# Batch 0's first maxima moved ahead of batch 1's set-up, six transfers moved to ScalarE, and the first experts' indirect transfers without bounds

## The reference, cut to what matters

```python
x = x + tanh(g_xattn[0]) * attention0(layernorm(x), ctx)   # 16 heads of 16, causal, softmax
x = x + tanh(g_ffn[0])   * experts0(layernorm(x))          # top 8 of 32 experts, 256 slots each
x = x + tanh(g_xattn[1]) * attention1(layernorm(x), ctx)   # 16 heads of 16, masked, softmax
x = x + tanh(g_ffn[1])   * experts1(layernorm(x))          # top 2 of 8 experts, 1024 slots each
```

## Time and profile before

| what | value |
|---|---|
| median of 3 executions | 1957.07 us |
| the profiled execution's own time | 1959.72 us |
| its span | 1958.0 us |
| PE busy | 1784.8 us (91%) |
| DVE, ACT, POOL busy | 1006.0, 887.7, 788.7 us |
| granted TensorE clock, mean | 0.97 |
| first attention | span from 0 to about 580 us |
| first experts | about 580 to 828 us |
| second attention, second experts | from 828 us to the end |

### The profile page before, as it was taken

One profiled execution on the slowest core, in us unless ns is written; L12 is line 12 of the kernel. 1 busy time (PEld: TensorE's weight loads), 2 busy tenths in 40 slices (PEclk: granted clock), 3 DMA queues, 4 the chain that ended last, 5 costly groups with the idle time before them and its releaser, 6 DMA issues. The chain is left out here.

```text
span 1958.0 us, 31351 instructions
## 1 busy us (share of the span) xinstructions
PE 1784.8 (91%) x11109; PEld 1094.3 (56%) x11109; DVE 1006.0 (51%) x2638; ACT 887.7 (45%) x1684; POOL 788.7 (40%) x772
## 2 busy tenths in 40 slices
PE   7799999999858999588999999999967999999997
PEld 5456656665547777443344444433344766766675
DVE  4656666677556444238677777777521222212211
ACT  4466666665603222155777778766731111111110
POOL 4211667766626777531114124211133134433323
PEclk9999999999969999799999999999988999999999
DMA  5554555643317887444333343231132133333314
GB/s 163 164 180 152 149 162 151 178 109 117 113 44 188 167 176 166 80 142 134 110 107 111 103 131 106 81 119 52 55 104 93 21 80 87 85 81 83 73 29 133
DMA packets 210331, 224.10 MB, mean 114 GB/s; under 512 B 40048, under 2 KB 200818, under 8 KB 209511
## 3 DMA queue, kind: packets, MB, share of 16 engines
q1 hardware_dynamic: 176490, 177.54, 30.1%
q0 software_dynamic: 33408, 44.69, 12.1%
q10 hardware_dynamic: 288, 0.00, 0.0%
HBM read 156.14 MB, written 87.06 MB: 124 GB/s over the span
## 5 line engine op out<-in xcount | busy, mean ns | idle before, releaser
L1001 DVE TENSOR_REDUCE nmx<-mxb 128x1 f32<-128x512 f32 (+2 forms) x866 | 502.2, 609 | 249.6 <-PE mxb L737 128.5
L838 ACT ACTIVATE pt<-stb 128x512 f32<-128x512 f32 x832 | 474.0, 600 | 247.7 <-PE stb L753 120.6
L734 PE MATMUL mxb<-kst,qst 96*128 96x512 bf16 (+2 forms) x986 | 318.4, 344 | 18.3 <-DVE nmx L1001 14.7
L753 PE MATMUL stb<-qst,kst 99*128 99x512 bf16 (+4 forms) x1024 | 326.7, 342 | 5.8 <-DMA qst<-m3T 3.3
L769 PE MATMUL ob<-pt,va 128*32 128x512 f32 (+3 forms) x2048 | 219.4, 523 | 2.5 <-ACT pt L838 1.7
L753 PEld LDWEIGHTS stb<-qst,kst 102*128 102x128 bf16 (+1 forms) x1024 | 99.4, 98 | 214.4 <-ACT pt L838 130.7
L1358 POOL DMA_INDIRECT slots<-number,place x192 | 189.3, 986 | 58.6 <-issue 58.5
L1328 POOL TENSOR_TENSOR qk<-qk,parts 128x512 f32<-128x512 f32 x60 | 68.5, 1165 | 314.2 <-ACT qk L877 204.4
L1897 POOL DMA_INDIRECT x_after_l<-e_y,e_token x56 | 87.2, 1558 | 242.7 <-DVE e_y L1862 229.3
L734 PEld LDWEIGHTS mxb<-kst,qst 99*128 99x128 bf16 (+1 forms) x986 | 96.7, 98 | 118.1 <-DVE nmx L1001 58.1
L1650 POOL DMA_INDIRECT x_after_l<-e_y,token x64 | 102.5, 1601 | 50.4 <-DMA x_after_l<-e_y,token 23.2
(11 more groups left out here) (280 smaller groups left out, 3013.9 us busy)
## 6 DMA issues: line engine op xcount, KB each, us to landing
kst<-qk_parts SPq DMA_DIRECT2D x384, 64.0 KB, 2.3
qst<-qk_parts SPq DMA_DIRECT2D x384, 64.0 KB, 2.3
qk_parts<-parts SPq DMA_DIRECT2D x14, 1536.0 KB, 6.5
rows<-rows SPq DMA_DIRECT2D x15, 1060.0 KB
crow<-in_ctx SPq DMA_DIRECT2D x16, 512.0 KB, 4.0
x_after_l<-xres SPq DMA_DIRECT2D x16, 512.0 KB, 3.3
e_gu_nat<-in_L_ffn_gate_up_proj SPq DMA_DIRECT2D x64, 128.0 KB
qst<-in_L_ffn_w SPq DMA_DIRECT2D x8, 1024.0 KB, 6.7
```

The costliest lines, as they stand in the source:

```text
L734: last = pe.matmul(out, qst[par][0:rows_used, h, qt * P:(qt + 1) * P], kst[par][0:rows_used, h, 0:nk], start=True, stop=not causal)
L753: last = pe.matmul(bank[:, to:to + S - q_from(kt)], kst[par][0:ROWS, h, kt * P:(kt + 1) * P], qst[par][0:ROWS, h, q_from(kt):S], start=Tru ...
L838: act.activation(pt[:, slot(b, u), q0:S], stb[no % N_ST][:, q0:S], ACT.Exp, scale=SCALE).then_inc(s["st_free"], 1)
L1001: last = dve.tensor_reduce(nmx[:, qt, h:h + 1], got[:, at:at + k_to(qt)], AX.X, ALU.max, negate=True)
```

## The change

It has five parts.

1. **Maxima earlier.** `filling(it, u)` gives the steps of batch 0's maxima that are done at step u. In iteration -2 these are 0 to 4 at step 8 (`AHEAD = 5`), and one more at every fourth step from 27 on, up to 14 at step 63 (`FILLED = 15`). In iteration -1 the steps 15 to 50 are spread evenly over all 64 steps. PE and DVE both follow it. Before, all 51 stood from step 13 of iteration -1 on. In layer 0 only 5 of every 8 steps have a bank, in layer 1 all have.
2. **`set_up_bias`** goes from step 14 to step 6 of iteration -2 on DVE.
3. **Half a stack by ACT.** The six `qst` transfers of `stack(0, 0)` are issued by ACT in front of its loop, which waits for `parts_out` (batch 0's q parts have landed) for them. SP skips them.
4. **The first shift by ACT.** The three transfers of `shift(0, 0)` are issued by ACT right behind its copy to `m3T`, not by SP behind `stack(1, 0)`.
5. **No bounds.** The 64 gathers and 64 adding scatters of experts0 lose `bounds_check` and `oob_is_err`, and with them the write of the limit to a register ahead of each. Parts 1, 3 and 4 apply to both attention layers.

```diff
--- before.py
+++ after.py
@@ -221,6 +221,8 @@
 BANK = {(kind, t): bank for kind, _, t, _, bank in TRIPS.values()}
 STEPS = 64
 BEHIND = 13
+AHEAD = 5
+FILLED = AHEAD + 10
 N_HI = SLOTS // P
 
 LISTED = 6
@@ -444,6 +446,14 @@
                 return ring[i % len(ring)], i - len(ring) + 1
             return mxb[i % N_MX], N_MAX * n + i - N_MX + 1
 
+        def filling(it, u):
+            if it == -2:
+                return range(0, AHEAD) if u == 8 else range(AHEAD + (u - 24) // 4, AHEAD + (u - 23) // 4) if u >= 24 else ()
+            if it == -1:
+                share = STEPS - BEHIND - FILLED
+                return range(FILLED + share * u // STEPS, FILLED + share * (u + 1) // STEPS)
+            return ()
+
         def rows_of(b):
             return slice(b * S, (b + 1) * S)
 
@@ -501,6 +511,8 @@
                 sp.wait_ge(s["k_out"], 16)
                 wait(sp, s["st_full"], N_SCORE * (n - 2) + N_SCORE // GROUPS * (g + 1))
                 for side, dst, terms in ((1, kst, K_TERM), (0, qst, Q_TERM)):
+                    if side == 0 and n == 0 and g == 0:
+                        continue
                     if side == 0 or n > 0:
                         sp.wait_ge(s["parts_out"], 16 * (n + 1))
                     for r, term in enumerate(terms):
@@ -576,8 +588,6 @@
                 if nn is not None:
                     parts_store(nn)
                     stack(nn, 0)
-                if nxt == 0:
-                    shift(nxt, 0)
                 if prev is not None:
                     store(prev)
                 if nn is not None:
@@ -807,8 +817,10 @@
                         scores(cur, u)
                     if u < BEHIND and cur is not None:
                         maxima(cur, u + STEPS - BEHIND)
-                    if u >= BEHIND and nxt is not None:
+                    if u >= BEHIND and nxt:
                         maxima(nxt, u - BEHIND)
+                    for first_u in filling(it, u):
+                        maxima(0, first_u)
                     for call, at in enumerate(sorted(VALUE_CALLS)):
                         if u == at - 16 and prev is not None:
                             values(prev, GROUPS - 1, call)
@@ -917,6 +929,11 @@
                     act.wait_ge(a.w_ones, 32)
                     act.wait_ge(a.w_ones1, 32)
                 act.activation(m3T[hf][:, :], bank_of("shift", hf)[0:3 * HALF, :], ACT.Copy).then_inc(evac["shift"], 1)
+                if n == 0 and hf == 0:
+                    act.wait_ge(evac["shift"], 1)
+                    for r in range(3):
+                        act.dma_start(qst[0][ROW_SHIFT + r:ROW_SHIFT + r + 1, 0:HALF, :],
+                                      m3T[0][HALF * r:HALF * (r + 1), :]).then_inc(s["shift_in0"], 16)
 
             def route(b):
                 act.wait_ge(s["lg_rdy"], b + 1)
@@ -940,6 +957,10 @@
             middle(0, 0)
             evacuate("v", 0, 0)
             evacuate("v", 0, 1)
+            act.wait_ge(s["parts_out"], 16)
+            for r, term in enumerate(Q_TERM):
+                act.dma_start(qst[0][DH * r:DH * r + DH, 0:4, :],
+                              qk_dram[0][0, term].rearrange("(h d) s -> d h s", d=DH)[:, 0:4, :]).then_inc(stack_in[0][0], 16)
             for it in ITERATIONS:
                 prev, cur, nxt, nn, n3 = (item(it, k) for k in range(-1, 4))
                 nn = nn or None
@@ -1229,12 +1250,16 @@
             for it in ITERATIONS:
                 done, prev, cur, nxt, nn, n3 = (item(it, k) for k in range(-2, 4))
                 for u in range(STEPS):
-                    if layer == 0 and it == -2 and u == 14:
+                    if layer == 0 and it == -2 and u == 6:
                         set_up_bias()
                     if u < BEHIND and cur is not None and u + STEPS - BEHIND in MAX_BANKS:
                         maxima(cur, u + STEPS - BEHIND)
-                    if u >= BEHIND and nxt is not None and u - BEHIND in MAX_BANKS:
+                    if u >= BEHIND and nxt and u - BEHIND in MAX_BANKS:
                         maxima(nxt, u - BEHIND)
+                    if it < 0:
+                        for first_u in filling(it, u):
+                            if first_u in MAX_BANKS:
+                                maxima(0, first_u)
                     if layer == 0 and done is not None and done >= LISTED:
                         if u in ONE_HOT_AT:
                             one_hot(done, ONE_HOT_AT.index(u) // 4, ONE_HOT_AT.index(u) % 4)
@@ -1639,8 +1664,7 @@
                 wait(pool, s["x_full"], e - N_ROW + 1)
                 for i in range(TILES):
                     pool.indirect_dma_start(row[e % N_ROW][:, i, :], None, table,
-                                            bass.IndirectOffsetOnAxis(token[:, TILES * e + i:TILES * e + i + 1], 0),
-                                            bounds_check=T + CAP0 - 1, oob_is_err=True).then_inc(rows_in[e % N_ROW], 16)
+                                            bass.IndirectOffsetOnAxis(token[:, TILES * e + i:TILES * e + i + 1], 0)).then_inc(rows_in[e % N_ROW], 16)
 
             def add(e):
                 if e > 0:
@@ -1648,7 +1672,7 @@
                 pool.wait_ge(s["y_done"], e + 1)
                 for i in range(TILES):
                     pool.indirect_dma_start(x, bass.IndirectOffsetOnAxis(token[:, TILES * e + i:TILES * e + i + 1], 0), y[e % 3][:, i, :], None,
-                                            bounds_check=T + SPARE - 1, oob_is_err=True, compute_op=ALU.add).then_inc(added[e % 2], 16)
+                                            compute_op=ALU.add).then_inc(added[e % 2], 16)
 
             for e in range(AHEAD):
                 gather(e)
```

## The result

| | before | after |
|---|---|---|
| median | 1957.92 us (6 runs, 1954.91 to 1960.56) | 1968.05 us (6 runs, 1964.29 to 1968.83) |
| ratio after / before | | 1.0042, 95% interval 1.0028 to 1.0057 |
| profiled execution, its span | 1959.72, 1958.0 us | 1964.47, 1962.7 us |
| start to first scores, first attention | 82.1 us | 86.2 us |
| from there to the first gather of experts0 | 501.1 | 501.8 |

What follows compares the result with a forecast made beforehand. PE's waits bound the attention starts and POOL the first experts, by 0.55 us per expert. Terms +6 (first attention), +4 (second) and -6 (no bounds) made +4 us, forecast 1961 us against the median, range 1947 to 1969.

Steps and rivals of the forecast that it cites:

- what is late: Both attention starts: batch 1's statistics, x(1) and load_x(2) come late; x(1) by 12.8 and 15.0 us.
- Front 1: Start of the first attention up to its first scores: +6.0 us, from a later store landing less the shift's wait.
- The term between q(2)'s second half and the scores: First attention: 4.9 us from q(2)'s second half to the scores being ready but for the shift.
- ACT's three issues, some 1.4 us, lie in its wait for the store: First attention: ACT's issuing of the first shift fits into its waiting for parts_store(1).
- Front 2: Start of the second attention up to its first scores: +4 us, with parts_store(1) landed by 905.6.
- a bound of +8: Second attention's start: upper end of the loss, whose range was 0 to +8 us around +4.
- Rival C: Both attention starts: the store lands earlier, at 78.3, fronts cost +2.4; 1953.5 us in all; chance 0.12.
- No bounds, -6 forecast: First experts on POOL: dropping the index test saves 0.1 us per scatter, two scatters, 31 rounds: -6 us.
- Two scatters, 0.1 us each: First experts: each adding scatter on POOL gets 0.1 us shorter without the test and its register write.
- A faster gather would gain nothing: First experts: an add's landing takes as long as the two gathers, 3.06 against 3.10 us, so only adds shorten the round.
- Rival B: First experts: the test is dear, 0.25 us per scatter, -15.5 us, bringing POOL to PE's time; 1951.5 us; chance 0.20.
- rival A: First experts: the test costs nothing, leaving only the late batch 1 at +10; 1967 us; chance 0.33.

Runs made afterwards that it cites:

- e3: The changed kernel with batch 1's statistics put ahead of the bias and the first maxima on DVE; 1946.86 us, ratio 0.9938 to the kernel before.
- e9: The changed kernel with the first five maxima's reductions behind batch 1's statistics on DVE, bias still ahead in layer 0; 1953.19 us, ratio 0.9973 to before.
- e8: The changed kernel with load_x(2) issued behind stack(0, 3) on SP, statistics still late; 1970.95 us, ratio 1.0063 to the kernel before.
- e10: e3 with the six qst transfers of stack(0, 0) issued by SP again; 1950.12 us, ratio 0.9949 to the kernel before.
- e7: The kernel before with only the first shift issued by ACT and no bounds (parts 4 and 5); 1945.26 us, ratio 0.9930.
- e2: The changed kernel with the bounds put back (parts 1 to 4 alone); 1973.41 us, ratio 1.0076 to the kernel before.
- e1: The kernel before with the bounds removed from gathers and adding scatters (part 5 alone); 1950.48 us, ratio 0.9955.
- e5: The kernel before with the bounds removed from the 64 gathers of the first experts alone; 1957.73 us, ratio 0.9999.
- e4: The kernel before with only the first shift issued by ACT (part 4 alone); 1952.70 us, ratio 0.9967.
- e6: The kernel before with the bounds removed from the 64 adding scatters of the first experts alone; 1954.35 us, ratio 0.9975.

## Why the prediction was right and wrong

**Right: what is late.** That DVE's list would put batch 1's statistics behind the bias and the reductions, the start at 38 to 40 us (39.01), x(1) 12.8 and 15.0 us later (13.1 and 15.1), SP held at `load_x(2)` to 44.7 (44.87), the store landed at 81.9 (81.87) and q(2)'s second half at 83.2 (83.38) all came as worked out. e3 and, for the second attention, e9 show that this is the cause of the loss. In the first attention the bias alone holds the statistics to 36.27 (e9) and the maxima alone would have held them about as long, since their stack lands only at 36.6; no run takes the early bias out by itself.

**Front 1, +6.0 forecast, +4.1 in the trace.** The term between q(2)'s second half and the scores was 4.9 us, taken over from before, where the first two multiplications ran at half rate (2.08 in the earlier trace rows). In after they took 1.12 and 1.07 and the term was 2.8. The step "ACT's three issues, some 1.4 us, lie in its wait for the store" was mis-sized: they take 2.57 us and only just fit (81.95 against 81.87). In e3, e8, e9 and e10 they stick out. Against what this front could be with the shift by ACT (e7, 76.87) it is 9.3 us too long: 6.2 for the late statistics (against e3) and 3.05 between e3 and e7. In e7 the shift's turn comes at 66.33, and ACT has issued the shift (67.37 to 69.94) before the store lands at 72.33; in e3 the turn comes at 72.11, about as late as the landing, behind the maxima that were put in front of x(1).

**Front 2, +4 forecast, +11.3 in the trace.** This is the step that failed. Forecast was a store at 70.7 us into the phase, landed at 77.2, scores 5.3 later; measured 72.3, 79.2 and 10.3 later. I took the store as what binds and 4 of the first attention's 4.9 us behind it. But when it landed PE still had batch 1's v, the shift's turn (904.05), q(2) and the maxima between in its list. From x(1) to the first scores PE needs 49.5 us in before and 45.7 in after. So x(1) 15.1 us late, less 3.8 for the maxima done earlier, is 11.3. The same list of PE took 43.6 us in e3 and e9; the change's 45.7 go with a granted clock of 0.50 in 68 to 76 us of the phase, where those two have 1.00. I had put a bound of +8 on this; the bound of 15 that the lateness itself gives stood in the text but not in the term.

**What the early maxima are worth.** The table gives it for both fronts. Behind x(1) they save: 45.2 us to the scores in e7, 41.9 in e3 in the first attention, 51.0 against 43.6 in the second. Ahead of x(1) they cost, even with the statistics first, since PE takes them in order and they wait for the first stack to land: x(1) 31.7 becomes 38.0, and 28.8 becomes 36.0. The sums are +3.0 and -0.2. The second is flattered by e7's clock: in e7's second attention the first four multiplications of q(2) took 1.92 and 1.71 us for each two, in e3's 1.02 and 1.02, which is 1.6 us. e7, which has neither the early maxima nor the half stack, is not slower than e3, which has both. Rival C (the late chain does not bind) had the store landed at 78.3 and the fronts at +2.4; the store landed at 81.87 and e2 is at +14.9.

**No bounds, -6 forecast, -11.2 in the trace, -8.8 alone by the ratio.** The size is not shown to be off (the interval of e1 holds 6), but the mechanism was wrong. "Two scatters, 0.1 us each" is measured as nothing at the issue (1.63 and 1.59) and 0.5 us at the landing. "A faster gather would gain nothing" holds for gathers alone (e5), not behind faster landings. PE did not become the bound: the round stayed at 6.43, above its 6.07. Rival B, with 15.5 us, was farther off than the forecast by the ratio and put the gain at the issue too, where there was none. The Trainium skill (GPSIMD Engine Reference, elementwise cycle accounting) reckons about 12 cycles per element for branches that depend on data; no bounded transfer here shows the 1.28 us that the prediction estimated from it for 128 indices: a gather shows 0.07 us, the landing of the adds 0.5.

**The sum.** +4 forecast, +8.2 by the ratio. In the traces the terms were off by -1.9 (front 1), +7.3 (front 2) and -5.2 (bounds), which nearly cancel; by the ratios of e2 and e1 by +4.9 and -2.8. That the range held the result is owed to this cancelling, so it is luck in part; with the fronts at their measured size and the term for the bounds as it was, the sum would have said slower. The single time nearest to the result was rival A's, 1967, and that is luck altogether: A has no gain from the bounds and +10 for the fronts, and e1 and e2 measured -8.8 and +14.9.

**Open.** Where the other 3 to 4 us of e4's gain come from. What the half stack is worth. What the early bias costs by itself. Whether `bounds_check`, `oob_is_err` or the write of the limit to a register carries the 0.07 and the 0.5 us; every run takes all three away together. And what sets PE's granted clock: the second attention's front is 79.5 and 79.8 us in e1 and e7 and 78.0 to 78.2 in before, e4, e5 and e6, and the difference stands in four multiplications of q(2), which took 1.91 and 1.64 us in e1, 1.92 and 1.71 in e7, and 1.02 and 1.02 in the others (granted clock 0.73 and 0.71 in 68 to 76 us of the phase, 1.00 in the others). So a front read from one trace can be 1 to 2 us off for the clock alone.

## What to carry to other kernels

When work is moved ahead to fill idle time, ask what stands behind it on every engine that takes part, above all the one that isn't the bound: here five reductions of 0.6 us, put ahead of nine small instructions on an engine that is half idle, held the normalisation, a load, and the whole front of the second attention, and mostly by what they waited for (11.79 us) rather than by their own 3 us; in the first attention the bias, put ahead as well, stood before them for most of that time. With the start of the longest chain first on DVE, 20 us of the change came back (e3); the first attention is even then 3 us behind the kernel that left the maxima where they were (e7). And in front of a phase count from the start of the chain to its end on the engine that carries it, not from the last transfer seen to bind.

## What the runs showed that I had not expected

- The bounds on an adding scatter cost nothing at the issue (mean 1601 ns with, 1621 without) and 0.5 us at the landing (2.96 to 3.17 against 2.46 to 2.74). On a gather they cost 0.07 to 0.08 us of POOL's issue.
- Transfers issued by one engine delay those issued by another. With SP's next stack beside ACT's half stack (e8), the first stack was complete 3.8 us later in the second attention, while ACT's six issues hardly changed (3.34 against 3.30 us in the first). The Trainium skill (DMA: Bandwidth & Descriptors, on issuing engines not being separate DMA queues) says that issuing from several engines saves only the issuing time; the traces agree: here the stack's landing moved, and e3, where ACT takes some 3 us of issuing from SP, has fronts 1.7 and 1.3 us shorter than e10.
- Three transfers of the shift cost ACT 2.57 us of issuing, 0.86 each. SP's six of a stack take 2.77, 0.46 each.
- PE behind a long wait can show the lower granted clock for some microseconds: 0.60 in 36 to 45 us of after, with its wait of 7.27 us, 1.00 there in before, and 1.09 us are four of x(1)'s transposes instead of eight. A wait can cost more than its length, but not each does: behind 3.17 us e7 ran at full rate, behind 2.89 e4 at half.
